# Output projection folded into the values: (V Wo) instead of (attention x V) Wo, in a one-core attention and gated feed-forward kernel

## The reference

```python
q = relu(x @ Wq + bq); k = relu(x @ Wk + bk); v = relu(x @ Wv + bv)
e = einsum('bqd,bkd->bqk', q, k) / sqrt(D) - NEG * causal
attn = exp(e - max(e)); attn = attn / sum(attn)
y = einsum('bqk,bkd->bqd', attn, v)
return relu(y @ Wo + bo)
```

## Time and profile before

| | |
|---|---|
| time, median of 3 runs | 2360.76 us (2356.63 to 2360.77) |
| span of the profiled execution | 2354.9 us |
| its own time | not listed apart from the runs; the median lies 5.9 us above the span |
| mean granted TensorE clock | 0.967 |
| PE busy | 91% (x10581 matmuls) |
| DVE, ACT, POOL busy | 69%, 51%, 39% |

### The profile page before, as it was taken

The page is one execution under the profiler, slowest core; times in us unless marked ns, Lnnn a source line. Parts: engine busy times, 40 slices in busy tenths (PEclk is TensorE's granted clock), DMA queues, the critical chain, the costliest instruction groups (busy, mean ns, idle before and its releaser), DMA issues. The chain is left out here.

```text
span 2354.9 us, 38531 instructions
## 1 busy us (share of the span) xinstructions
PE 2134.7 (91%) x10581; PEld 1058.4 (45%) x10581; DVE 1636.5 (69%) x3637; ACT 1198.6 (51%) x2482; POOL 909.1 (39%) x1126
## 2 busy tenths in 40 slices
PE   5999999999999999999999999965888887888985
PEld 2445555445555444555544555532333333433432
DVE  6745656664654774565666465577999999999994
ACT  3443323444333344332344433234888888878876
POOL 1102211201211210211120021124899989998998
PEclk9999999999999999999999999996999999999998
DMA  4101112100111210111210011122322222222232
GB/s 144 54 23 48 56 39 84 53 32 30 61 47 54 73 54 23 43 52 48 74 62 32 25 55 59 54 77 95 90 85 84 82 85 89 77 88 87 76 94 76
DMA packets 91009, 151.20 MB, mean 64 GB/s; under 512 B 9538, under 2 KB 27074, under 8 KB 90820
## 3 DMA queue, kind: packets, MB, share of 16 engines
q1 hardware_dynamic: 90820, 149.05, 19.7%
HBM read 86.36 MB, written 62.65 MB: 63 GB/s over the span
## 5 line engine op out<-in xcount | busy, mean ns | idle before, releaser
L453 PE MATMUL psum<-v,work 128*128 128x512 f16 x1632 | 371.5, 379 | 1.2 <-DVE work L709 0.8
L453 PE MATMUL psum<-kT,qT 128*128 128x512 f16 (+3 forms) x1920 | 362.8, 347 | 0.0
L453 PE MATMUL psum<-work,w_hi 128*128 128x512 f16 x1024 | 309.6, 384 | 11.5 <-ACT xcT L628 7.5
L590 ACT ACTIVATE work<-psum 128x512 f16<-128x512 f32 (+2 forms) x228 | 125.3, 552 | 341.3 <-PE psum L537 298.2
L943 POOL TENSOR_SCALAR ve<-mv 128x1 f32<-128x1 f32 x66 | 14.7, 223 | 691.9 <-DVE mv L768 691.9
L453 PEld LDWEIGHTS psum<-kT,qT 128*128 128x128 f16 x1920 | 181.0, 98 | 171.1
L709 DVE SCALAR_TENSOR_TENSOR work<-psum,work 128x512 f16<-128x512 f32 (+2 forms) x228 | 143.3, 628 | 152.9 <-ACT work L590 150.3
L1326 DVE MAX8 c<-cut 128x8 f32<-128x512 f32 x384 | 243.9, 675 | 0.0
L453 PEld LDWEIGHTS psum<-v,work 128*128 128x128 f16 x1632 | 158.6, 98 | 171.1 <-DVE work L709 4.1
L1110 PE MATMUL psum<-fw,xsT 128*128 128x512 f16 x792 | 208.8, 420 | 1.1 <-ACT xsT L1212 1.1
L453 PE MATMUL psum<-work,w_lo 128*128 128x512 f16 x512 | 196.5, 384 | 0.0
(11 more groups left out here) (147 smaller groups left out, 4283.1 us busy)
## 6 DMA issues: line engine op xcount, KB each, us to landing
work<-x SPq DMA_DIRECT2D x72, 256.0 KB, 3.1
out<-zn SPq DMA_DIRECT2D x70, 256.0 KB, 3.0
h_scratch<-hb SPq DMA_DIRECT2D x68, 256.0 KB, 2.3
x<-x_scratch SPq DMA_DIRECT2D x66, 256.0 KB, 2.8
x_scratch<-xr SPq DMA_DIRECT2D x65, 256.0 KB, 2.1
h<-h_scratch SPq DMA_DIRECT2D x65, 256.0 KB, 3.7
xr<-x SPq DMA_DIRECT2D x64, 256.0 KB, 2.7
xc_scratch<-xcT SPq DMA_DIRECT2D x68, 128.0 KB, 2.1
```

The lines of the kernel that those rows point to most:

```text
L453: mm = nc.tensor.matmul(outp, stat(a), mov(c), start=(n == 0 and k == 0), stop=(n == total - 1 and k == 2))
L590: nc.scalar.activation(dst, src, ACT.Copy, scale=scale).then_inc(t_hi.sem, 1)
```

## The change

v is now made transposed (`vT`, like k and q), and multiplied by Wo in the projection stage (`vo`, 4 steps a group), so that attention weights times (V Wo) is the projected output at once. The bias and 1/sum are applied by `bias_o` straight from the y bank. The transposes `yT`, their two halves, `yn` and the steps `o` are gone. What came for tile t = i - 3 comes for u = i - 2, so everything behind it moves one step earlier, and the attention stage has 18 steps.

```diff
         def attention_steps(i):
-            u, t = i - 2, i - 3
+            u = i - 2
...
-            if 0 <= t < TILES:
-                yield ("yT", t)
...
-            if 0 <= t < TILES - 1:
-                yield ("o", t)
-            if 0 <= i - 7 < TILES - 4:
-                yield ("x", i - 7)
+            if 0 <= i - 6 < TILES - 4:
+                yield ("x", i - 6)
...
             for g in range(GROUPS):
+                for c in range(C):
+                    yield ("v", g, c)
...
-                if g == 0:
-                    yield ("o", -1)
                 for j in range(GROUP):
-                    yield ("v", g, j)
+                    yield ("vo", g, j)
...
-            for i in range(TILES + 3):
+            for i in range(TILES + 2):
...
+                def hi_vo(b, g, j):
+                    t = GROUP * g + j
+                    act.wait_ge(vo_ps.sem, vo_ps.at(b, t))
+                    nc.scalar.activation(v[:, 0, t, :], m_bank(("vo", g, j)), ACT.Copy, scale=V_DOWN).then_inc(vo_hi.sem, 1)
...
-                            act.wait_ge(y_ps.sem, y_ps.at(b, u))
-                            act.wait_ge(rcp_ok.sem, rcp_ok.at(b, u))
-                            nc.scalar.activation(yn[:], Y_BANK[u % 2], ACT.Copy, scale=rcp[:, u % 2:u % 2 + 1]) \
-                                .then_inc(yn_ok.sem, 1)
...
+                def lo_vo(b, g, j):
                     t = GROUP * g + j
...
+                    nc.vector.scalar_tensor_tensor(v[:, 1, t, :], m_bank(("vo", g, j)), V_DOWN, v[:, 0, t, :], ALU.mult, ALU.subtract) \
+                        .then_inc(vo_lo.sem, 1)
...
                 def bias_o(b, t):
 
-                    dve.wait_ge(o_ps.sem, o_ps.at(b, t))
+                    dve.wait_ge(y_ps.sem, y_ps.at(b, t))
+                    dve.wait_ge(rcp_ok.sem, rcp_ok.at(b, t))
                     dve.wait_ge(x1_ok.sem, x1_ok.at(b, t - 2))
-                    nc.vector.scalar_tensor_tensor(ob[:, t % 2, :], m_bank(("o", t)), O_DOWN, bo_b[:], ALU.mult, ALU.add) \
+                    nc.vector.scalar_tensor_tensor(ob[:, t % 2, :], Y_BANK[t % 2], rcp[:, t % 2:t % 2 + 1], bo_b[:], ALU.mult, ALU.add) \
                         .then_inc(o_ev.sem, 1)
...
                         between = []
-                        if 0 <= i - 6 < TILES:
...
                         if 0 <= i - 5 < TILES:
-                            between.append(lambda: residual_stats(b, i - 5))
-                        if 0 <= i - 4 < TILES and i >= TILES:
-                            between.insert(0, lambda: attention_stats(b, i - 4))
+                            between += [lambda: second_norm(b, i - 5), lambda: convolution(b, i - 5, 0),
+                                        lambda: convolution(b, i - 5, 1)]
+                        if 0 <= i - 4 < TILES:
+                            between.append(lambda: residual_stats(b, i - 4))
```

More of the change, by code:

```diff
@@ L467, in take_m @@
                     return m_bank(step)
-                def output_projection(b, t, bank):
-                    last = t_place["yT", t % TILES] - (T_ITEMS if t < 0 else 0)
-                    pe.wait_ge(t_lo.sem, t_lo.at(b, last))
-                    for n in range(C):
-                        mm = three(bank, n, C, lambda a: yT[:, a, n, :], lambda a: (w_hi, w_lo)[a][:, 3, n, :])
-                    mm.then_inc(o_ps.sem, 1)
                 def conv_transposes(b, t, bank):
@@ L853, in _ @@
                         late_tiles(b, g)
-                        bias_v(b, g, 0)
-                        for j in range(1, GROUP):
-                            bias_v(b, g, j)
-                            lo_v(b, GROUP * g + j - 1)
-                        lo_v(b, GROUP * g + GROUP - 1)
+                        for j in range(GROUP):
+                            lo_vo(b, g, j)
                     conv_stats(b, -1)
-                    for i in range(TILES + 3):
-                        u, t = i - 2, i - 3
-                        if 0 <= i - 4 < TILES and i < TILES:
-                            attention_stats(b, i - 4)
+                    for i in range(TILES + 2):
+                        u = i - 2
+                        if 0 <= i - 3 < TILES and i < TILES:
+                            attention_stats(b, i - 3)
                         if i < TILES:
@@ L881, in _ @@
                         between = []
[L882 to L884 removed]
                         if 0 <= i - 5 < TILES:
[L886 to L888 removed]
+                            between += [lambda: second_norm(b, i - 5), lambda: convolution(b, i - 5, 0),
+                                        lambda: convolution(b, i - 5, 1)]
+                        if 0 <= i - 4 < TILES:
+                            between.append(lambda: residual_stats(b, i - 4))
+                        if 0 <= i - 3 < TILES and i >= TILES:
+                            between.insert(0, lambda: attention_stats(b, i - 3))
                         if i == TILES:
@@ L902, in _ @@
                             later()
-                        if 0 <= t < TILES - 1:
-                            bias_o(b, t)
-                        if 0 <= i - 8 < TILES:
-                            conv_stats(b, i - 8)
+                        if 0 <= u < TILES - 1:
+                            bias_o(b, u)
+                        if 0 <= i - 7 < TILES:
+                            conv_stats(b, i - 7)
                 for g in range(GROUPS):
@@ L1463 @@
         "wqkvo": np.stack([a("attn_W" + w) for w in "qkvo"]),
-        "bqk": np.ascontiguousarray(np.stack([columns(a("attn_b" + w)) for w in "qk"], 1)),
-        "bv": rows(a("attn_bv")), "bo": rows(a("attn_bo")),
+        "bqkv": np.ascontiguousarray(np.stack([columns(a("attn_b" + w)) for w in "qkv"], 1)),
+        "bo": rows(a("attn_bo")),
         "ffw": a("ffn_weight"), "ffb": rows(a("ffn_bias")),
```

234 lines of the change are left out of this document (101 added, 133 removed).

## The result

| | before | changed |
|---|---|---|
| median of 20 runs each | 2357.8 us | 2362.89 us |
| lowest, highest | 2354.37, 2361.77 | 2356.79, 2366.29 |
| span of the profiled execution | 2354.9 us | 2361.0 us |

The ratio is 1.0016, with a 95% interval of 1.0009 to 1.0023: slower by 0.16%, which is small but clear of the noise, and within the 0.2% that the prediction called no change. The forecast was 2380 us, some 20 us more than before; 5 more were measured. The time of a run lies 2.0 us above its span (2362.97 against 2361.0 for the profiled one).

The account below looks back on a forecast made before the run. PE's own instruction stream was taken to bound the attention loop. Loop +22.5, tail -8.7 and clock +6 gave +19.8 us on the 2354.9 span, 2374.7; with 5.9 from span to median, 2380 us, range 2356 to 2392.

Parts of the forecast that it names:

- What the cover was, steps 6 to 10: Attention steps 6 to 10: lost PE cover exposes DVE's chain, waits of 0.7 to 2.9 us, 8.9 us per batch.
- End of a batch: Steps 16 and 17 of each batch: longer PE waits, +1.4 and +4.4, together +5.8 us.
- Start of stage, projection: Projection start: wait before first `pT` 0.9 us shorter, 4.7 us of `ln_norm` waits gone, `late_tiles` covered.
- Per batch: Loop: -7.0 + 8.9 + 5.8 - 0.9 = +6.8 us per batch; four +27, less 4.7: +22.5.
- The lengths of the stages: Per batch: attention stage some 32 us shorter, projection 39 us longer, no wait in steps 11 to 15.
- The clock: Step 17: its wait brings one more PE clock fall per batch, 4 x 1.5 = 6 us; upper bound 17.
- The start-up: Start of the kernel: one POOL clear less and one DVE clear more, counted as nothing.
- The tail: Between loop and feed-forward: last `bias_o` 12.1 us earlier, 3.4 of it already counted, so -8.7 us.
- The feed-forward stage should keep its 754 us: Feed-forward stage behind the tail: unchanged at 754 us; if not, something else moved.
- Rival 1: Attention loop: cover not needed, PE stays dense, no clock falls, 2316 us; chance 0.13.
- Rival 2: Turn of the batch: step 17's delay disappears there (-8), no clock fall added (-6), 2366 us; chance 0.15.
- Rival 3: Steps 6 to 10: each gap brings a clock fall, and `late_tiles` delays `vo`, 2394 us; chance 0.12.

Follow-up runs that it names:

- end-of-batch run: Changed kernel with DVE's order altered only in steps 16 and 17 (`bias_o(14)` earlier, three pieces moved later): 2340.83 us, 0.9915 of the kernel before.
- the run with the clears first: Changed kernel with POOL's buffer clears at the very start, ahead of the first `ln_scale`: 2359.14 us, 0.9995 of the kernel before.
- the run with double work: Changed kernel with the 12 matmuls of the first chunk of the scores done twice in steps 6 to 10: 2379.24 us, 1.0087 of the kernel before.
- the one with all reorderings: Changed kernel with three edits of DVE's order, clears first, and two pieces ahead of the lo half in step 5: 2298.93 us, 0.9737 of the kernel before.

## Why the prediction came out as it did

It had the mechanism and the sizes of the waits right, and was wrong in the total: 19.8 us more were forecast, 6.1 came in the two profiled executions and 5.1 between the medians. What failed are terms outside the attention steps: the start-up, which it counted as nothing (2.6 us less, the most of 3.3 in the first batch), the feed-forward stage, which it held fixed (5.2 us less), and the last batch with the tail (4.4 us less). The clock term was too small as well, but that was made up by shorter waits. By its own steps:

- **What the cover was, steps 6 to 10: right.** Forecast were 65.2 us from `pT(4,0)` to `pT(9,0)`, measured 288.64 - 223.78 = 64.9; the first chunk was put at T+8.7 and came at T+8.80. The waits of the first batch (2.83, 2.07, 1.64, 1.17, 0.55, each with the 0.16) are 8.3 against 8.9; where the clock had fallen in step 6, in batches 2 and 4, step 7 waited 0.6 only. Two things in it were wrong by themselves. The slack of 1.47 was 2.09 at least. And in front of step 6 the changed order adds nothing, since all four pieces stood behind `pT(4,0)` before too: that wait is the cover's alone. Neither did harm, as the step lengths were built on the changed order itself.
- **End of a batch: right.** Waits of 0.92, 1.69, 0.92 and 4.83 in steps 16 and 17 against 0.69, 0.36 and 1.33 before: +6.0, forecast +5.8. The end-of-batch run took the largest of them away, and the clock falls behind it, for 22 us in all.
- **Start of stage, projection: right.** The wait before the first `pT` fell by 0.8 (forecast 0.9), the waits for `ln_norm` went, and no `vo` waits for `late_tiles`.
- **Per batch: right.** Turn to turn, the second and third batch are 5.9 and 6.8 us longer; the forecast's terms give 6.8 + 1.5 for the clock - 1.6 for `ln_norm` = 6.7.
- **The lengths of the stages: right.** In batch 2 the projection, from the turn of the loop to the first `pT`, is 35.5 us longer (forecast 39 for the steps alone) and the rest up to the next turn 29.6 us shorter (forecast some 32), and no wait lies in steps 11 to 15.
- **The clock: too small.** Low stretches lie at step 17 of all four batches, at step 6 of batches 2 and 4 and at one turn, 7 in place of 3. That is the forecast's count of four more, by luck in part: it had none at step 6, and two of the old places lost theirs. Matmuls inside them lost 15.0 us against 4.6, worked out from their starts, so 10.4 more and not 6; a stretch at step 17 cost 2.3 to 2.9 us, not 1.5. Shorter waits at two of the turns (2.09 for 2.90, 1.82 for 2.53) and at step 7 of two batches gave back about the 4.4 us between.
- **The start-up, "I count nothing": failed.** The first `hT` comes at 17.1 in place of 19.4 us and the first matmul of the projection at 27.8 in place of 30.3. x landed 1 us earlier behind one constant less, and POOL's clears, which hold up DVE's `ln_norm` as the run with the clears first shows, are one fewer. (In the other two kernels with the old start the first `hT` came at 18.5 and 18.6, so some of this is scatter.) The first batch ended 5.0 us later and not 8.3: 3.3 us of error.
- **The tail: too small.** From the last `hT` to the first feed-forward matmul it is 38.5 us against 52.2, 13.7 less where 12.1 were forecast: the last `bias_o` starts 2.3 us behind the last `hT`, less than the 2.5 that the forecast had as the least; and the last batch up to that `hT` was 7.3 longer, not 10.1 (its old wait for `ln_norm` was 2.9, above the mean of 1.6). Together 4.4 us.
- **"The feed-forward stage should keep its 754 us": failed,** the largest single term of the error: 734.0 against 739.2 us by the same cut, -5.2. The seven turns of DVE's loop are 5.7 us shorter in sum, since DVE stands less long for its second piece of code. The change shifted where that code lies; 16 idle instructions alone move the same stage by 11.
- **The base.** 5.9 us stood between span and time, from a median of three runs; it is 2.0 for the profiled execution. That is 3.9 us of the forecast time, and none of the difference.

The sum for the span: 19.8 - 3.3 (first batch) - 0.8 (second batch) + 0.1 (third) - 4.4 (last batch and tail) - 5.2 = 6.2, and the spans differ by 6.1. The small terms nearly all erred to one side, and together they were 13.6 us, more than twice the effect. This sum is of one execution of each kernel, and single executions of the changed kernel lay between 2356.8 and 2366.3 us: that it comes out to 0.1 is no proof of every term.

Rival 1, that the cover was not needed, fell: the run with double work shows the waits filling up, and the one with all reorderings shows what it would have been. Its price was near: forecast were 45 us less, and that run is some 51 less than the kernel before without the clears and the feed-forward stage. Rival 2 said that step 17's delay disappears in the turn; the run for the end of the batch got 4.1 of its 4.7 us back in each batch, so it had not. Its clue was half right: the turn waits do give a little. Rival 3's clock falls behind step 6 came in two batches of four.

## What to carry to other kernels

When work leaves a stream that waits for nobody, ask what it covered, and lay out the chain of the other engine across the hole: the PE work taken out here came back as waits until the order on DVE was changed with it, and then the same change was worth some 2.2%. Before costing the effect itself, list what else the edit touches: constants and clears at the start, the tail, and where code lies. Differences of up to half a per cent between programs of different length can be the place of the code (2293.5 to 2306.6 us here); a few copies with some idle instructions in front tell how much.

## What the runs showed that I had not expected

- Sixteen waits on a semaphore long reached, ahead of a loop, moved the feed-forward stage from 739.2 to 727.8 us in one kernel and from 732.8 to 744.0 in another. At the turns of DVE's loop there pass 5.94 to 8.2 us (9.35 once) between the same two searches, for the same instructions, and the difference is how long DVE stands for the second of two packets of code.
- DVE's four `ln_norm` took 7.08 us beside POOL's clears and 1.92 alone.
- A wait in step 6 that brought a clock fall shortened the next wait (0.57 for 2.07): PE at the lower clock came later to it by itself. The fall's matmuls lost 1.7 us, and 1.5 of them came back there.
- In the three kernels with all reorderings PE had no wait over 2.1 us behind the start-up (with the 0.16), and its clock fell nowhere in the loop. In the kernel before it fell behind waits of 2.9, 2.6 and 2.9 us and not behind one of 2.5; the shortest wait in the loop of any run with a fall behind it was 2.2.
